# Eight instead of five of twelve context tiles as three rounded products, in a fused decoder layer

## The reference

```python
x = _layernorm(x + _L0_attn_ref(x, ...), axis=-1)
x = _layernorm(x + _L0_xattn_ref(x, ctx_1024, ...), axis=-1)
x = _layernorm(x + _L0_ffn_ref(x, ...), axis=-1)

def _L0_xattn_ref(hidden_states, encoder_hidden_states, Wq, Wk, Wv, Wo, gq, gk):
    ...
    q = rmsnorm((hidden_states @ Wq).reshape(B, Sq, H, D), gq)
    k = rmsnorm((encoder_hidden_states @ Wk).reshape(B, Skv, H, D), gk)
    v = (encoder_hidden_states @ Wv).reshape(B, Skv, H, D)
    scores = jnp.einsum('bqhd,bkhd->bhqk', q, k) * scale
    attn = jax.nn.softmax(scores, axis=-1)
    out = jnp.einsum('bhqk,bkhd->bqhd', attn, v)
    return out.reshape(B, Sq, H * D) @ Wo
```

## Time and profile before

| what | value |
|---|---|
| median of three runs | 1332.13 us (1331.4 to 1332.43) |
| the profiled execution | 1332.16 us |
| its span | 1330.4 us |
| granted TensorE clock over the span | 0.995 |
| PE busy | 1307.7 us, 98% |
| DVE, ACT, POOL busy | 1103.6, 1024.2, 1047.4 us (83%, 77%, 79%) |

### The profile page before, as it was taken

How to read it: one execution, slowest core, us unless ns; L and a number is a source line. 1 busy time by engine, 2 the same in 40 slices (tenths; PEclk the granted TensorE clock), 3 DMA queues, 4 the chain that set the end, 5 groups by cost and what they waited for, 6 DMA issues and landing times.

```text
span 1330.4 us, 25166 instructions
## 1 busy us (share of the span) xinstructions
PE 1307.7 (98%) x6366; PEld 1034.0 (78%) x6366; DVE 1103.6 (83%) x1715; ACT 1024.2 (77%) x3155; POOL 1047.4 (79%) x968
## 2 busy tenths in 40 slices
PE   8989999999999999999999999999999999999998
PEld 5767677777777777777777777777777777778787
DVE  5866689888888888888888888888888888896675
ACT  2667788888888888888888888888888888873442
POOL 5644442898989898989898988889888989898840
PEclk9989999999999999999999999999999999999999
DMA  7140230000000101010101010101010101030210
GB/s 252 50 156 1 83 131 19 29 17 31 17 32 13 37 12 35 12 36 12 35 12 36 12 35 10 38 8 39 8 40 8 39 8 39 1 111 1 88 50 29
DMA packets 27849, 53.96 MB, mean 41 GB/s; under 512 B 2816, under 2 KB 22400, under 8 KB 25936
## 3 DMA queue, kind: packets, MB, share of 16 engines
q1 hardware_dynamic: 26736, 52.38, 11.7%
q10 hardware_dynamic: 992, 0.36, 0.1%
HBM read 44.60 MB, written 8.13 MB: 40 GB/s over the span
## 4 chain that ended last, share of the span: by engine, by line
PE 92%; DVE 5%; issue 1%; ACT 1%; POOL 1%; DVEq 0%; ACTq 0%
PE xa_k_ps L1376 13%; PE xa_k_ps L1377 13%; PE xa_k_ps L1378 13%; PE xa_o_ps L1465 13%; PE xa_s_ps L1378 6%; PE xa_s_ps L1377 6%; PE xa_s_ps L1376 6%; PE om_ps L1471 3%; PE xa_o_ps L1376 2%; PE xa_o_ps L1377 2%; PE xa_o_ps L1378 2%; PE xq_ps L634 2%; DVE xa_ss L1304 1%; PE xa_o_ps L1393 1%; PE xa_o_ps L1401 1%
## 5 line engine op out<-in xcount | busy, mean ns | idle before, releaser
L1376 PE MATMUL xa_k_ps<-wk_parts,xa_ctxT_hi 128*125 128x512 f32 x768 | 376.5, 490 | 1.2 <-ACT xa_sq L1224 1.0
L1304 DVE TENSOR_REDUCE xa_ss<-xa_sq 125x6 f32<-125x768 f32 x360 | 339.7, 944 | 1.5 <-ACT xa_sq L1224 1.2
L1292 DVE TENSOR_TENSOR xa_scores<-xa_s_ps,xa_rk 125x448 f32<-125x448 f32 x384 | 238.6, 621 | 98.8 <-PE xa_s_ps L1378 97.0
L1377 PE MATMUL xa_k_ps<-wk_parts,xa_ctxT_hi 128*125 128x512 f32 x768 | 303.1, 395 | 0.0
L1378 PE MATMUL xa_k_ps<-wk_parts,ctxT_lo 128*125 128x512 f32 x768 | 302.3, 394 | 0.0
L1135 POOL TENSOR_TENSOR xa_den<-probs,xa_den 125x896 f32<-125x896 f32 x128 | 272.1, 2126 | 3.6 <-ACT probs L1209 3.6
L1209 ACT ACTIVATE probs<-xa_scores 125x896 f32<-125x896 f32 x192 | 183.6, 956 | 102.4 <-DVE xa_scores L1332 37.0
L1189 ACT ACTIVATE xa_sq<-xa_k_ps 125x512 f32<-125x512 f32 x360 | 212.2, 590 | 38.3 <-PE xa_k_ps L1378 21.7
L1223 ACT ACTIVATE xa_k_ps<-xa_k_ps 125x128 f32<-125x128 f32 x720 | 189.1, 263 | 31.2 <-PE xa_k_ps L1378 29.2
L1465 PE MATMUL xa_o_ps<-probs,xa_ctx_nat 125*128 125x448 f32 x448 | 205.4, 539 | 0.0
L1312 DVE TENSOR_TENSOR xa_max_ps<-xa_scores,xa_max_ps 125x448 f32<-125x448 f32 x320 | 198.3, 620 | 0.6
(11 more groups left out here) (186 smaller groups left out, 2360.9 us busy)
## 6 DMA issues: line engine op xcount, KB each, us to landing
xa_ctx_nat<-in_ctx SPq DMA_DIRECT2D x16, 750.0 KB
ctxT_in<-in_ctxT SPq DMA_DIRECT2D x84, 125.0 KB, 2.0
qo<-in_xo_w SPq DMA_DIRECT2D x1, 2048.0 KB, 16.0
qo<-in_xq_w SPq DMA_DIRECT2D x1, 2048.0 KB, 15.6
vo_scratch<-qo SPq DMA_DIRECT2D x2, 1024.0 KB, 4.6
w_parts_scratch<-ws_hi SPq DMA_DIRECT2D x2, 1024.0 KB, 4.1
w_parts_scratch<-ws_lo SPq DMA_DIRECT2D x2, 1024.0 KB, 5.4
vo<-vo_scratch SPq DMA_DIRECT2D x1, 2048.0 KB, 8.4
```

The costliest lines, as they stand in the source:

```text
L1292: dve.tensor_tensor(scores[0:KP, j, :, :], raw, key_scale, ALU.mult).then_inc(s_taken, 1)
L1304: dve.tensor_reduce(ss[:, i // 2, UH * (i % 2):UH * (i % 2) + vector_heads(of)], squares(of, i).rearrange("p (g d) -> p g d", d=XD), AX.X, ...
L1376: pe.matmul(out, l_hi, r_hi, start=first, stop=False)
L1377: pe.matmul(out, l_hi, r_lo, start=False, stop=False)
```

## The change

Which tiles are split is now a table for each pair of tiles: none of pair 0, both of pair 1, the odd one of pairs 2 and 3, both of pairs 4 and 5, so tiles 2, 3, 5, 7, 8, 9, 10 and 11. The last context keeps the five tiles of before (`LAST_SPLITS`). `xa_p_hi` has room for both tiles of a pair, and the rounded context has one place of eight tiles instead of two of five; its parts are made in steps 17 and 21 (high) and 18 and 23 (low) instead of 8, 9, 12 and 13. The tile products come one step later (`PV_LAG` 21), the denominators too (`TD` 9), the scores have 20 slots instead of 24. DVE shifts pairs 0, 2, 4 and 6 in steps t = 2, 4, 6 and 8, POOL pairs 8 and 10, and each engine counts its shifts on a semaphore of its own. All contexts are written out; there is no loop.

```diff
-def each_phase(eng, body, loop_end):
+def each_phase(body):
-    for b in (-1, 0, 1):
-        body(Phase(b))
-    with eng.Fori(1, loop_end // 2) as pair:
...
+    for b in range(-1, B + 1):
         body(Phase(b))
-PV_LAG = EXP_LAG + 5
+PV_LAG = EXP_LAG + 6
-TD = 8
+TD = 9
+VECTOR_SHIFTS = {2: 0, 4: 2, 6: 4, 8: 6}
+VS, GS = 4, 2
+PAIR_SPLITS = (0, 2, 1, 1, 2, 2)
+LAST_SPLITS = (0, 1, 1, 1, 1, 1)
+NAT_PARTS = slice(2, 4), slice(5, 6), slice(7, 12)
+NAT_HI_AT = {17: (0, 1), 21: (2,)}
+NAT_LO_AT = {18: (0, 1), 23: (2,)}
+SC = 20
...
-                                           p_hi[:, y // 2 % (NPR // 2), :].bitcast(F32), ALU.subtract
+                        first = 2 - split_tiles(ph, y)
+                        slots = slice(y % NPR + first, y % NPR + 2)
+                        pool.tensor_tensor(probs_r[0:KP, slots, :], probs[0:KP, slots, :],
+                                           p_hi[:, y // 2 % (NPR // 2), first:2, :].bitcast(F32), ALU.subtract
...
+                        if split_tiles(ph, y) == 2:
+                            act.activation(p_hi[:, y // 2 % (NPR // 2), :, :], score_pair(ph, y), ACT.Exp
                                            ).then_inc(p_hi_ready, 1)
...
-                    y = lagged_pair(ph, j, SHIFT_LAG)
-                    pairs = [y] if y is not None and vector_shifts(y) else []
+                    pairs = [KT * (h - 1) + VECTOR_SHIFTS[t]] if t in VECTOR_SHIFTS and ended_half(ph, h) else []
...
-                            pe.wait_ge(shift_done, ph.at(STEPS, y + (KT if ph.b == B else KT // 2)))
+                            pe.wait_ge(vector_shifted, vector_shifts_done(ph, y + KT - 2))
...
+                        for part, tiles in enumerate(nat_parts(of)):
+                            if hy == 0 and ty == tiles.start:
+                                pe.wait_ge(nat_lo_ready, of.at(len(NAT_PARTS), part + 1))
-                        if ty % 2 and ty > 1:
+                        if ty % 2 >= 2 - split_tiles(ph, y):
```

More of the change, by code:

```diff
@@ L869, in adds_done, with vector_shifts_done, pool_shifts_done, tiles_of @@
     return ph.at(2 * ADDS, ADDS * half + max(k, 1))
+VECTOR_SHIFTS = {2: 0, 4: 2, 6: 4, 8: 6}
+VS, GS = 4, 2
 def vector_shifts(y):
-    return y % KT < KT // 2
+    return y % KT < 2 * VS
+def vector_shifts_done(ph, y):
+    last = ph.b + y // STEPS == B - 1 and y // KT % 2
+    return ph.at(2 * VS, VS * (y // KT) + (y % KT // 2 + 1 if last else min(y % KT // 2 + 1, VS)))
+def pool_shifts_done(ph, y):
+    return ph.at(2 * GS, GS * (y // KT) + y % KT // 2 + 1 - VS)
+PAIR_SPLITS = (0, 2, 1, 1, 2, 2)
+SPLIT_TILES = [2 * i + o for i, n in enumerate(PAIR_SPLITS) for o in range(2 - n, 2)]
+LAST_SPLITS = (0, 1, 1, 1, 1, 1)
+NAT_PARTS = slice(2, 4), slice(5, 6), slice(7, 12)
+LAST_PARTS = slice(3, 6, 2), slice(7, 8), slice(9, 12, 2)
+NAT_ENDS = 4, 6, KT
+def tiles_of(part):
+    return list(range(KT))[part]
+def split_tiles(ph, y):
+    return (LAST_SPLITS if ph.b + y // STEPS == B - 1 else PAIR_SPLITS)[y % KT // 2]
+def nat_parts(ph):
+    return LAST_PARTS if ph.b == B - 1 else NAT_PARTS
+def nat_place(ph, tile):
+    return [t for part in nat_parts(ph) for t in tiles_of(part)].index(tile)
+NAT_HI_AT = {17: (0, 1), 21: (2,)}
+NAT_LO_AT = {18: (0, 1), 23: (2,)}
+SC = 20
 SPLIT_PAIRS = KT // 2 - 1
@@ L891, in early_products @@
         first, last = 3 * (j - 4), 3 * (j - 3)
[L892 removed]
+    elif ph.b == B and j < EARLY_STEPS:
         first, last = 3 * (STEPS - 4) + 2 * j, 3 * (STEPS - 4) + 2 * (j + 1)
@@ L969, in spread_pair, with nat_part, nat_hi_part @@
             return o_ps[0:KP, (y // KT) % 2, 0:UW].unsqueeze(1).broadcast_to([KP, 2, UW])
[L971 to L977, removed]
+        def nat_part(nat, ph, part):
+            return nat[:, ph.parity(), nat_parts(ph)[part], :]
+        def nat_hi_part(ph, part):
+            tiles = tiles_of(nat_parts(ph)[part])
+            at = nat_place(ph, tiles[0])
+            return nat_hi[:, at:at + len(tiles), :]
         def probs_pair(y):
@@ L1204, in body @@
                     if y is not None:
-                        wait(act, shift_done, ph.at(STEPS, y + 2))
+                        if vector_shifts(y) or ph.b == B and y >= -KT:
+                            act.wait_ge(vector_shifted, vector_shifts_done(ph, y))
+                        else:
+                            act.wait_ge(pool_shifted, pool_shifts_done(ph, y))
                         wait(act, pv_done, ph.at(STEPS, y - NPR + 2))
@@ L1208, in body @@
                             wait(act, den_done, adds_done(ph, y - NPR))
-                        act.activation(probs_pair(y), score_pair(y), ACT.Exp).then_inc(exp_done, 2)
-                        if y % KT:
-                            act.activation(p_hi[:, y // 2 % (NPR // 2), :], score_slot(y + 1), ACT.Exp
+                        act.activation(probs_pair(y), score_pair(ph, y), ACT.Exp).then_inc(exp_done, 2)
+                        if split_tiles(ph, y) == 2:
+                            act.activation(p_hi[:, y // 2 % (NPR // 2), :, :], score_pair(ph, y), ACT.Exp
                                            ).then_inc(p_hi_ready, 1)
[L1213 to L1216, removed]
+                        elif y % KT:
+                            act.activation(p_hi[:, y // 2 % (NPR // 2), 1, :], score_slot(ph, y + 1), ACT.Exp
+                                           ).then_inc(p_hi_ready, 1)
+                    if ph.within(0, 15):
+                        for part in NAT_HI_AT.get(j, ()):
+                            act.wait_ge(nat_loaded[ph.parity()], nat_loads(ph))
+                            wait(act, pv_done, ph.at(STEPS, NAT_ENDS[part] - KT))
+                            act.activation(nat_hi_part(ph, part), nat_part(ctx_nat, ph, part), ACT.Copy).then_inc(nat_hi_ready, 1)
                     if ph.within(-1, 14):
```

89 lines of the change are left out of this document (42 added, 47 removed).

## The result

The changed kernel takes 1337.76 us (median of 6 runs, 1337.41 to 1340.5) against 1331.5 us for the kernel before on the same chip: ratio 1.0048, 95% interval 1.0037 to 1.0059. It is slower by 0.48%, where I had forecast no change. The profiled execution took 1337.59 us, its span is 1335.4 us, 5.0 longer than before's 1330.4.

The account below looks back on a forecast made before the run. PE, busy 98% of the span, was taken as the bound. From 1332.16 us, -13.5 (shorter products) +8.8 (boundary) +1.3 (step 17) +2.0 (start) gave 1330.8 us, "the same"; the range went from 1322 to nearly 1337.

Parts of the forecast that it names:

- when POOL's row starts: Before two contexts meet: POOL's row begins 7.41 us after step 18's first key product, following ACT's rounding of the denominators.
- the boundary: Where two contexts meet: step 3's key product waits 0.63 us for ACT behind POOL, in 14 contexts, +8.8 us.
- the end: Last context: one tile product moves a step later, behind the early products; POOL has 5.9 us free; costs nothing.
- PE's gain of 0.15 us a tile: PE's tile products: a split tile takes 0.61 us, a whole one 0.76; 90 tiles give -13.5 us.
- the fourth shift: Rival, 0.04: DVE's added shift delays the tile product of t = 9, costing 18 us, 1348.8; 0.27 us to spare.
- The row is longer: Rival, 0.19: at the contexts' boundary POOL's and ACT's upper bounds hold, 1.16 us a boundary, 1338.2 us.
- Step 17: ACT's exponentials, copies and squares make PE wait 0.09 us in 14 contexts, +1.3 us.
- Step 21: ACT's closing of a half, exponential and five tiles: PE's 0.09 us wait falls inside the next one, adding nothing.
- The start: Context 0: products of step 20 a step later and more ACT work, between 0 and 2.3, taken as +2.0 us.
- Writing-out worth nothing: All contexts: written-out form and removed loop register instructions have no share of their own, as contexts 1 and 4 match.
- the sign that I had named as being wrong: In the new profile: DVE's shift seen as releaser of PE would show the forecast wrong; no size given.

Follow-up runs that it names:

- the last variants: Changed kernel with eight split tiles kept, low part late and copies early: 1323.95 us; with five split tiles in context 14 too: 1321.98 us.
- all three edits: Changed kernel with POOL's five-tile low part behind the last shift, ACT's two copies in step 15, and five split tiles in context 14 too: 1321.98 us, ratio 0.9924.
- the first experiment: Kernel before with its contexts written out and nothing else changed: 1331.53 us, ratio 0.9998.
- the second: Changed kernel with five split tiles in every context, the rest of the change kept: 1333.03 us, ratio 1.0008.

## Why the prediction was wrong, point by point

In the profiled executions the change cost 1337.59 - 1332.16 = 5.4 us, where my sum has -1.4. Two of its terms failed: when POOL's row starts, which sizes the wait at the boundary, and the end, which I had put at nothing. By its steps:

- **PE's gain of 0.15 us a tile: right.** Contexts of five splits take 67.33 us, those of eight in the last variants 66.51, of which 0.09 is a wait in step 22 (see step 21 below): (67.33 - 66.42) / 6 = 0.151 us. For 90 tiles that is 13.6 us. The Trainium skill ("FP8 and Floating Point Precision", section TensorE Precision Notes) says that true FP32 takes four passes; the estimate of 0.187 us that I drew from it is above this figure, and the measurement decides.
- **The boundary: right in place, mechanism and POOL's row, wrong in when the row starts.** The step that failed reads, word for word: "ACT's exponential of an odd step started 4.60 us after the first key product of the step before (292.33 to 296.93), because a shift of DVE ends just ahead of it". I took this time from a trace in which DVE did not wait there, and kept it although I was adding 0.9 us to ACT's step 17, whose squares DVE sums ahead of the shift. The row began 0.5 us later than with the copies or the shift moved; with either of them it began when I had said (7.41 us after a key product, whose load is some 0.2 us earlier: 7.61, measured 7.60 and 7.57). The wait is 0.94 us in place of 0.63, in 13 contexts and not 14, since context 15 has no keys: about +12.2 us for +8.8. Of the 0.5 us, 0.3 shows in this difference; the rest is covered by PE's own way from step 18 to step 3, which takes 25.38 us in the variant with the low part late, 0.17 more than my 25.21. When I weighed the fourth shift I did ask what a late DVE would do, and set it aside with "nothing new stands ahead of it on DVE": nothing new did, but the old sum of squares had something new to wait for.
- **"The row is longer" (1338.2) gave nearly the right time for a wrong reason.** None of its upper bounds came true; the row was not longer but later.
- **Step 17: 0.09 forecast, 0.04 found**, 0.5 us in place of 1.3. **Step 21:** I had a wait of 0.09 that would fall inside step 17's or the boundary's. It does not: steps 21 to 23 take 8.62 us where steps 9 to 11, with the same instructions on PE, take 8.53. 0.09 x 14 = 1.3 us. Together they are 1.8 us where I had 1.3.
- **The start: +2.0 forecast, +1.33 in context 0.** Steps 16 to 18 are 0.87 us longer than before: 0.46 comes from the copies (54.72 us with them in step 15), the rest from the wider rounded exponential, as I had counted (0.4 + 0.5). Steps 20 to 23 are 0.5 us longer, less than what I added for the product a step later and for ACT's five tiles.
- **The end: "Nothing" was wrong, by about 3 us.** With all three edits the stretch from context 14 on takes 213.04 us; with six tiles more split and the boundary's wait it would be 213.04 - 0.91 + 0.94 = 213.1, and the changed kernel takes 216.3, 3.2 more. I had argued with POOL's free time over the last context, an average; at its start POOL was still behind with context 14's low parts, now two tiles wide, while PE's steps had lost their keys. Five tiles in the last context came one context late to prevent it. That POOL's low parts are the cause is shown by the variant with five in context 14; how the 3 us divide between the waits listed (2.7 us, of which the kernel before has 0.4 too) and the rest is not. Another 0.5 us is the schedule's, as the variant with five splits everywhere shows: from the last product of scores to the last tile product it takes 34.4 us, before 33.7. The tile product that I moved "behind the early products" for nothing lengthens this tail.
- **Writing-out worth nothing: right**, by the first experiment. **The fourth shift not in PE's way: right in contexts 1 to 13**, by the second, but not in context 0: the weights of step 21's product wait 0.68 us for it in the changed kernel, the sign that I had named as being wrong. It is part of the 0.5 us of steps 20 to 23.

Together: -13.6 + 12.2 + 0.5 + 1.3 + 1.3 + 3.2 + 0.5 = +5.4 us. That this is the measured figure is partly luck: the span grew by 5.0 us, with the stretch ahead of context 0 shorter by 0.3 (187.4 for 187.7 us, which varies from one profile to the next), and 0.4 us lie outside the span (2.2 for 1.8).

## What to carry to other kernels

When a step gains work on one engine, follow every engine that waits for its output until the path comes back to the first one: here ACT delayed DVE by 0.39 us, DVE delayed ACT, ACT delayed POOL, and POOL ACT and PE. A time "after the step's start" that was read from the old trace holds only as long as what stands ahead of it does not begin to wait. Then look at the order on the engine that is late before cutting its work: a part that nobody needs yet, done behind the one that everybody waits for, gave 12.1 us with no instruction less. And where the work per step changes, at the first and last context, free time averaged over a context did not tell what one engine still had to finish: the low parts that it hid elsewhere cost 3 us there.

## What the runs showed of the hardware

A wait of PE in context 0 cost its clock in some executions and not in others. Windows of PE (stretch, its length, PE busy with instructions, granted clock, DMA share, GB/s) in the profile of the variant with DVE's shift first:
```profile
226.00:228.00 2.00, 0.60 (x3) 1.00 0.00 0
228.00:230.00 2.00, 1.51 (x4) 0.63 0.00 0
230.00:232.00 2.00, 2.00 (x7) 0.52 0.00 0
232.00:236.00 4.00, 4.00 (x20) 1.00 0.38 118
```
PE's load of keys had waited 2.34 us, from 226.15 to 228.49, and the clock stood at the lower level, 1.2 GHz, for the next 3 to 4 us; loads then follow each other at 0.37 to 0.43 us in place of 0.20 to 0.25, and context 0 takes 56.06 us in place of 55.18. The variant with five tiles in context 14 shows the same behind a wait of 2.33 us (0.50 in the window from 230). The changed kernel's own profile has a wait of 2.35 us at the same place, that of the variant with the low part late one of 2.34, and both stay at 1.00. What makes the difference is not shown. It adds about 0.9 us now and then, and I left context 0 out when comparing the later contexts of the two that have it.
